# Residual cells made from both sides on TensorE in a cross-attention and spline-FFN kernel

## The reference

```python
def attn(teacher_logits, feat, Wq, bq, Wk, bk):
    query = einsum('bnc,dc->bnd', feat, Wq) + bq
    key = einsum('bnc,dc->bnd', feat, Wk) + bk
    attention = softmax(einsum('bnd,bmd->bnm', query, key))
    return einsum('bln,bmn->blm', teacher_logits, attention)

def spline(cp, out_size, in_size):   # p0..p3: four neighbouring control points, f: place between them
    w = 0.5 * (2*p1 + (p2-p0)*f + (2*p0-5*p1+4*p2-p3)*f**2 + (3*p1-p0-3*p2+p3)*f**3)
    return w.reshape(out_size, in_size)

x = x + attn(layernorm(x), ctx, Wq, bq, Wk, bk)
h = layernorm(x)
x = x + (silu(h @ gate_w.T) * (h @ up_w.T)) @ down_w.T
```

## Time and profile before

| | us |
|---|---|
| median of 3 runs | 286.06 |
| lowest and highest | 284.72, 287.19 |
| the profiled execution | 285.89 |
| its span | 283.9 |
| mean granted TensorE clock, share of full | 0.976 |

### The profile page before, as it was taken

The page is one execution under the profiler, slowest core; times in us unless marked ns, Lnnn a source line. Parts: engine busy times, 40 slices in busy tenths (PEclk is TensorE's granted clock), DMA queues, the critical chain, the costliest instruction groups (busy, mean ns, idle before and its releaser), DMA issues.

```text
span 283.9 us, 3824 instructions
## 1 busy us (share of the span) xinstructions
PE 263.8 (93%) x1250; PEld 168.4 (59%) x1252; DVE 182.0 (64%) x322; ACT 125.2 (44%) x202; POOL 132.9 (47%) x138
## 2 busy tenths in 40 slices
PE   7699479997999999999999999999999999599995
PEld 3232167763654858865548588755375888364674
DVE  0699977887457774764567838646587476464403
ACT  3044623325767702257767222557674133353300
POOL 0489462579653811309718123078083131594800
PEclk9959959999999999999999999999999999999999
DMA  6899044000720000032600000226000001100003
GB/s 188 312 424 409 2 131 168 0 2 0 267 105 0 3 0 0 2 148 90 279 0 0 0 0 0 94 76 274 0 0 0 0 0 74 74 0 2 0 0 148
DMA packets 7209, 23.23 MB, mean 82 GB/s; under 512 B 1184, under 2 KB 2336, under 8 KB 5792
## 3 DMA queue, kind: packets, MB, share of 16 engines
q1 hardware_dynamic: 7200, 23.11, 21.7%
HBM read 18.92 MB, written 4.19 MB: 81 GB/s over the span
## 4 chain that ended last, share of the span: by engine, by line
PE 73%; DVE 13%; ACT 5%; issue 4%; DMA 2%; POOL 1%; SPq 1%; ACTq 0%; DVEq 0%; POOLq 0%
PE bank L1304 11%; PE bank L1350 10%; PE bank L1306 9%; PE bank L1324 7%; PE bank L1157 5%; PE bank L1254 5%; PE bank L1255 4%; PE bank L1256 4%; PE bank L1168 4%; PE bank L1357 3%; DVE prod L856 3%; PE bank L1211 3%; DMA power<-in_g_power 2%; DVE prob L840 2%; DVE inter L947 1%
## 5 line engine op out<-in xcount | busy, mean ns | idle before, releaser
L1107 POOL TENSOR_TENSOR ih<-inter,ones 128x512 fp32r<-128x512 f32 x64 | 65.7, 1042 | 35.2 <-DVE inter L947 33.7
L947 DVE TENSOR_TENSOR inter<-inter,bank 128x512 f32<-128x512 f32 x64 | 43.4, 687 | 26.0 <-ACT inter L762 26.0
L762 ACT ACTIVATE inter<-bank 128x512 f32<-128x512 f32 x64 | 37.7, 599 | 25.1 <-PE bank L1306 24.5
L733 ACT ACTIVATE qk<-bank,nmr,rstd 128x512 f32<-128x512 f32 x16 | 12.5, 780 | 46.7 <-PE bank L1256 46.7
L1350 PEld LDWEIGHTS bank<-d_r,ih 128*128 128x128 f32 x256 | 30.6, 192 | 4.1 <-issue 3.2
L1304 PE MATMUL bank<-xh,gate_r 128*128 128x512 f32 x64 | 29.9, 467 | 1.5 <-DVE zg L939 1.5
L1350 PE MATMUL bank<-d_r,ih 128*128 128x192 f32 x256 | 31.1, 274 | 0.0
L1324 PE MATMUL bank<-inter,d_u 128*64 128x512 f32 x128 | 30.1, 602 | 0.0
L1304 PE MATMUL bank<-xh,up_r 128*128 128x512 f32 x64 | 27.2, 425 | 1.4 <-DVE inter L947 1.3
L1091 POOL TENSOR_TENSOR xres<-x,ones 128x2048 f32<-128x2048 f32 x4 | 14.4, 3602 | 23.9 <-DMA out<-xres 23.6
L1306 PE MATMUL bank<-zg,gate_v 102*128 102x512 f32 x64 | 25.3, 395 | 0.0
(11 more groups left out here) (100 smaller groups left out, 458.2 us busy)
## 6 DMA issues: line engine op xcount, KB each, us to landing
x<-in_x SPq DMA_DIRECT2D x4, 1024.0 KB, 4.8
xT<-in_xT SPq DMA_DIRECT2D x4, 1024.0 KB, 6.9
out<-xres SPq DMA_DIRECT2D x16, 256.0 KB, 2.1
ctxT<-in_ctxT SPq DMA_DIRECT2D x4, 512.0 KB, 7.6
rd<-in_d_r SPq DMA_DIRECT2D x2, 768.0 KB, 6.4
knots<-in_d_knot SPq DMA_DIRECT2D x1, 1280.0 KB, 12.1
d_coef<-in_d_coef SPq DMA_DIRECT2D x1, 1024.0 KB, 14.8
d_pt<-in_d_node SPq DMA_DIRECT2D x1, 1024.0 KB, 16.9
```

The source lines that it names most:

```text
L762: nc.scalar.activation(inter[:, m], gbank[m % 2][:], ACT.Silu).then_inc(s["silu_done"], 1)
L947: V.tensor_tensor(inter[:, m], inter[:, m], ubank[m % 2][:], ALU.mult).then_inc(s["mult_done"], 1)
L1107: G.tensor_tensor(ih[:, m], inter[:, m], ones[:, 0].broadcast_to([P, TOK]), ALU.mult).then_inc(s["ih_done"], 1)
```

## The change

- Each cell is now made as two polynomials, one for the side in front of the break and one for the side behind it, both by float32 products with 32 rows on TensorE (gate and up straight from `weighted`; down from a table `d_table` of factors times jumps). `residual` on VectorE is one `copy_predicated` within PSUM, by a loaded byte mask, and on ScalarE one copy into the weights. GpSimd has no part in it any more. `spread(r)` makes cells r and r + 1 in one step.
- The bf16 splits go. GpSimd makes the low part of `x` for batch 0 (`split_x0`), the tables (`tables`, six operations of 128x512) and all of `down_nodes`. `powers` moves to VectorE.
- `project` leaves the head of `ffn`. For batch 0 it stands in the prologue ahead of `residual(10)`; for batches 1 to 3 at the end of the turn before. `replicate` opens `ffn`; it no longer lies inside `qk`.
- `normalise` of the last tile is a step of its own (`normalise_last`). The prologue has another order with `qk(0)` first, four `keep_warm` of which none comes later, and the loads are in another order, context and query weights first. The loads `r2g`, `r3g`, `rd2`, `rd3`, `g_pick`, `d_spread` give way to `g_cell`, `g_after`, `d_table`, `d_shape`, `d_after`.

```diff
 def attention_only(st):
     st.constants()
...
+    for _ in range(4):
+        st.keep_warm(zdbank)
+    st.qk(0)
+    st.powers(0)
+    st.spread(0)
+    for t in range(2):
+        st.energy(0, t)
+    st.residual(0)
+    for t in range(2):
+        st.softmax(0, t)
+    for u in range(2):
+        st.node_product(u)
+    st.residual(1)
+    st.node_weights(0)
+    st.powers(1)
+    for t in range(2, 4):
+        st.energy(0, t)
+    st.softmax(0, 2)
+    st.node_weights(1)
+    st.softmax(0, 3)
+    st.spread(2)
+    for n in range(NT):
+        st.split_x0(n)
+    for u in range(2, 4):
+        st.node_product(u)
+    st.scale(0)
+    for t in range(2):
+        st.prob_t(0, t)
+    st.residual(2)
+    st.split_prob(0, 0)
+    st.residual(3)
+    st.split_prob(0, 1)
+    st.node_weights(2)
+    st.jump_inputs(0)
+    for t in range(2, 4):
+        st.prob_t(0, t)
+        st.split_prob(0, t)
+    st.spread(4)
+    st.node_weights(3)
+    st.stats(0)
+    st.xm(0, 0)
+    for u in range(4, 6):
+        st.node_product(u)
+    st.jump_inputs(1)
+    for r in range(4, 6):
+        st.residual(r)
+    st.mean_shift(0)
+    st.xm(0, 1)
+    st.spread(6)
+    st.node_weights(4)
+    st.add_xm(0, 0)
+    st.node_weights(5)
+    st.xm(0, 2)
+    st.jumps()
+    st.tables()
+    for u in range(6, 8):
+        st.node_product(u)
+    for r in range(6, 8):
+        st.residual(r)
+    st.add_xm(0, 1)
+    st.xm(0, 3)
+    for u in range(6, 8):
+        st.node_weights(u)
+    for t in range(2, 4):
+        st.add_xm(0, t)
+    st.spread(8)
+    st.residual(8)
+    st.normalise_last(0)
+    st.residual(9)
+    st.spread(10)
+    st.turn()
+    for t in range(4):
+        st.norm_t(0, t)
+        st.cast_t(0, t)
+    for k in range(4):
+        st.down_taps(k)
+    st.down_nodes()
+    st.project(0)
+    for r in range(10, 12):
+        st.residual(r)
+    st.spread(12)
+    for r in range(12, 14):
+        st.residual(r)
+    st.spread(14)
+    for r in range(14, 16):
+        st.residual(r)
 def ffn(st, b, a=None):
-    st.project(b)
-    if a is not None:
-        st.between(a)
-    else:
-        st.replicate(b)
+    st.replicate(b)
...
     if a is not None:
         st.cast_t(a, 3)
+        st.project(a)
# VectorE and ScalarE, residual
-    V.tensor_tensor(prod2[:, r % 2, k, 0:width], bank[2 * (r % 2) + k][:, 0:width], part[...], ALU.mult)  # k = 0, 1
+    V.copy_predicated(left, after, right).then_inc(s["picked"], 1)
+    act.wait_ge(s["picked"], r + 1)
+    nc.scalar.activation(dst, bank[2 * (r % 2)][:, 0:dst.shape[1]], ACT.Copy).then_inc(s["res_done"], 1)
# TensorE, spread
+    if r == 2 * CLS:
+        pe.wait_ge(s["table_done"], SIDES)
+        pe.wait_ge(s["shape_in"], 16)
+    for side in range(SIDES):
+        for q in (r, r + 1):
+            if side == 0 and q >= 2:
+                pe.wait_ge(s["res_done"], q - 1)
+            dst = bank[2 * (q % 2) + side]
+            if q < 2 * CLS:
+                c = slice(q % CLS * WROWS, (q % CLS + 1) * WROWS)
+                last = mm(dst[:], g_cell[c, side], weighted[c, q // CLS], start=True, stop=True)
+            else:
+                for n, m in enumerate(tile_pair(q)):
+                    w = m // CLS
+                    c = slice(QUAD * w, QUAD * (w + 1))
+                    last = mm(like_blocks(dst[:, n * STRIP:(n + 1) * STRIP], w), d_shape[c, side, m % CLS],
+                              in_blocks(d_table[c, 0, side], w), start=True, stop=True)
# GpSimd, tables
+    for k in range(2):
+        pool.wait_ge(s["jump_done"], k + 1)
+        for side in range(SIDES):
+            G.tensor_tensor(d_table[:, k, side], d_table[:, k, side], jump[:, k], ALU.mult)
+    for side in range(SIDES):
+        pool.wait_ge(s["table_mul"], 2 + side + 1)
+        G.tensor_tensor(d_table[:, 0, side], d_table[:, 0, side], d_table[:, 1, side], ALU.add)
```

More of the change, by code:

```diff
@@ L55 @@
 WIDTH = PERIOD / 4
-S2, S3 = 256.0, 2048.0
 EPS = 1e-5
@@ L154, in constants @@
     coef = np.zeros((CLS, WROWS, G_K))
+    cell_coef = np.zeros((CLS, POWERS, TAPS, SIDES, P))
+    after = np.zeros((P, CLS, HID), np.uint8)
     jump = {2: np.array([0.5, -1, 0, 1, -0.5]), 3: np.array([0.5, -2, 3, -2, 0.5])}
-    pick = np.zeros((CLS, POWERS, TAPS, 2, P))
-    r2, r3 = np.zeros((P, INTER)), np.zeros((P, INTER))
     for a in range(CLS):
         h = hidden[a * P:(a + 1) * P]
-        for n in range(4):
-            for k, scale in enumerate((S2, S3)):
-                pick[a, 0:2, n:n + 5, k] += jump[2 + k][:, None] / scale * (cell[h] // CLS == n)
         i = rows[a].ravel()
         place = ((knot[i] + (cell[h] // CLS)[:, None]) - start[i]) * PERIOD
-        left, right = nodes[cell[h]][:, None], nodes[cell[h] + 1][:, None]
-        r2[:, a * HID:(a + 1) * HID], r3[:, a * HID:(a + 1) * HID] = cell_residual(h[:, None], left, right, place)
+        left, right = nodes[cell[h]], nodes[cell[h] + 1]
+        if not ((place > left[:, None]) & (place < right[:, None])).all():
+            raise ValueError("a break outside its cell")
+        after[:, a] = h[:, None] > place
         phase = start[i] - knot[i]
@@ L170, in constants @@
         power[a] = ((phase - mid) / half) ** np.arange(POWERS)[:, None, None]
+        for j in range(P):
+            n = cell[h[j]] // CLS
+            for side, polys in enumerate(gate_cell(h[j], left[j], right[j], n, mid, half)):
+                for k, poly in enumerate(polys):
+                    cell_coef[a, 0:len(poly.coef), n:n + 5, side, j] += poly.coef[:, None] * jump[2 + k]
         for n in range(G_NODES):
@@ L370, in attention_only @@
-            for t in range(3, 7):
-                st.keep_warm(t)
-            for r in range(2):
-                st.spread(r)
+                st.softmax(0, t)
[10 more added lines that the diff above has]
+            st.spread(2)
@@ L1153, in qk @@
                     for n in range(2):
-                        if n == 1 and not first(b):
-                            Stages.replicate(b - 1)
                         for c in range(CTX // P):
@@ L1192, in spread @@
-                    for k in range(2):
-                        dst = bank[2 * (r % 2) + k]
-                        if r < 2 * CLS:
-                            c = slice(r % CLS * WROWS, (r % CLS + 1) * WROWS)
-                            last = mm(dst[:], pick[c, k], win_hl[c, r // CLS], start=True, stop=True)
-                        else:
-                            for n in range(2):
-                                m = 2 * (r - 2 * CLS) + n
-                                for part, row in pieces(dst[:, n * STRIP:(n + 1) * STRIP], jump[k], m // CLS):
-                                    last = mm(part, spread_[:, m], row, start=True, stop=True)
```

456 lines of the change are left out of this document (197 added, 259 removed).

## The result

| | before | changed |
|---|---|---|
| median of 4 runs, us | 286.6 | 309.3 |
| lowest and highest | 284.7, 287.2 | 308.0, 309.9 |
| ratio, 95% interval | | 1.081 (1.077 to 1.085) |
| profiled execution, its span | 285.89, 283.9 | 308.66, 306.6 |
| mean granted clock | 0.976 | 0.916 |

The direction was forecast, the size was not: 291.0 was said, and 309.3 lies outside 284.5 to 295.5. The span has grown by 22.7 us, 16.9 of them ahead of the first gate product and 5.8 behind it (212.7 us from there to the end before, 218.5 now).

A forecast was written before the change was run, and what follows sets the result against it. TensorE bounds the loop, hand-overs between engines the prologue. Span 283.9 + 2.0 (first gate product later, 1.3 of it clock) + 3.1 (heads of turns) = 289.0, plus 2.0 outside the span: 291.0 us, range 284.5 to 295.5.

The forecast's parts named there:

- ledger: Prologue: the queues run step by step in written order at full clock; first gate product at 71.9 us against 71.2.
- rival 3: Prologue picks: each costs 1.3 us instead of 0.69, source and target both in PSUM; time 297; chance 0.07.
- Rival 4: Prologue: the lead survives, first gate product at 67.0, time 284.8; chance 0.30, of which 0.12 more than 1% faster.
- The clock: Prologue: half clock behind TensorE gaps of 2.6 and 2.4 us; 1.3 us taken, ends 0 and 5.1.
- second fall: Prologue: half clock from the 2.4 us gap ahead of spread(10), on spread(10), transposes and project; about 2.7 us more.
- G: Start of the first gate product, end of the prologue: 71.2 us before, forecast 71.9 + 1.3 = 73.2.
- first fall: Prologue: half clock from the 2.6 us gap ahead of the transposes; 2.4 us passed on, half of it taken.
- The ledger of the middle: Prologue, 24 to 50 us: named likeliest error, if VectorE and ScalarE wait less for each other than counted.
- The port: Prologue: GpSimd's tables share a port pair with VectorE's additions of x and last jump; up to 1.4 us more.
- The heads of the turns: Loop, batches 1 and 2: TensorE idles 1.53 us each ahead of replicate, 3.06 in all; 3.1 taken.

The follow-up runs named there:

- e2: The run with fills: changed kernel plus 50 idle products of ones on TensorE in the five long gaps of the prologue; 301.3 us.
- e4: Changed kernel plus six idle products of ones on either side of replicate in batch 3; 305.8 us.
- e5: Changed kernel with replicate woven into qk again, GpSimd's low parts of x behind the scaling, idle products in batch 3 and the prologue; 294.9 us.
- e10: Changed kernel with replicate woven, low parts of x behind the scaling, tables early, last cells ahead of project, idle products at batch 3's head only; 294.9 us.
- e11: e10 plus idle products of ones in the prologue, around the node products, between the transposes and ahead of spread(10); 295.4 us.
- e7: Changed kernel with picks 10 and 11 and spread(12) directly behind spread(10), picks 12 and 13 among the transposes, spread(14) ahead of project; 301.5 us.
- e3: Changed kernel with one wait more: GpSimd begins the low parts of x only when VectorE has scaled the softmax; 304.3 us.
- e6: Kernel before with project moved to the end of the turn before and replicate at the head, no longer inside qk; 293.8 us.
- e12: e6 plus six idle products of ones ahead of each replicate and six more behind it in batch 3; 290.9 us.
- e13: Changed kernel with e3's wait, jump_inputs(1) directly behind jump_inputs(0), and GpSimd's down taps and down_nodes behind VectorE's low part of zp; 303.6 us.
- e14: e5 with 6 idle products in the first gap, the two additions of e13, and no idle products between the transposes; 294.4 us.

## Why the prediction was wrong

**The frame was right.** The kernel's loop is bound by TensorE, the prologue by hand-overs, and the loss comes from both. The ledger's first 21 us stand: `qk(0)` at 6.1 as said, the last exponential at 21.5 (21.9 said), a gate `spread` 1.99 (2.2), a down `spread` 2.04 at full clock (2.2), the pick 0.69 and 0.55 (0.69, 0.55; rival 3 falls). The picks held up by queue positions, `spread(8)` waiting for the tables and `spread(12)` for cells 10 and 11 are all in the timeline. Rival 4, the lead survives, falls: the scaling ended at 26.5 against a forecast of 23.9 and 37.05 before, a lead of 10.5 us in place of 13, and all of it was lost.

**The step that failed first is "The clock".** I priced it at 1.3 us with ends 0 and 5.1, "since one row can't say how short a gap is harmless". The run with fills measured 8.0, of which 6.9 are in the prologue, and e4 3.4 in batch 3, where I had not looked at all, since the kernel before went through the same gaps at full speed. Three things were missed. The gap of 2.6 us ahead of the transposes was 5.4. The second fall came behind another gap than the one I had: 3.0 us ahead of `spread(8)`, for the tables, where the ledger has 0.7, while ahead of `spread(10)` it was 1.3 and not 2.4. And a third, 2.5 us ahead of `spread(12)`, stands in my own ledger (59.7 to 62.5) and was not counted as one; what e2 won behind it, 5.2 us, is the largest part. Also I let each fall last some 7 us, as in the earlier trace rows (the second there ends at 42.2, by its row, not at 42.9). Here one fall lasted 17 us (22.7 to 39.7), with further gaps inside it, the second and third 13.6 each, so 44 of the 88 us ahead of G ran at half speed. The chain passes on only what lies on it: of the first fall, the one that I priced, at most 2.5 us (below).

**The ledger of the middle failed too.** I called 24 to 50 us the place where I was most likely wrong, but thought of shorter waits. VectorE's first statistics start at 34.68 and cell 9's pick ends at 62.81:

```profile
34.68 2.46 DVE L830 BATCH_NORM_STATS2 bst<-x 128x6 f32<-128x512 f32 x4
...
62.26 0.55 DVE L868 COPY_PREDICATED bank<-d_after,bank 128x384 f32<-128x384 uint8 x1
```

and in e5, whose clock was full through the whole stretch:

```profile
33.65 2.46 DVE L852 BATCH_NORM_STATS2 bst<-x 128x6 f32<-128x512 f32 x4
...
59.31 0.55 DVE L890 COPY_PREDICATED bank<-d_after,bank 128x384 f32<-128x384 uint8 x1
```

| us | ledger | changed | e2 | e5 | e10 | e11 |
|---|---|---|---|---|---|---|
| the scaling ends | 23.9 | 26.5 | 26.8 | 24.1 | 23.4 | 24.3 |
| end of the scaling to start of the statistics | 7.5 | 8.1 | 7.5 | 9.6 | | |
| start of the statistics to cell 9's pick | 22.1 | 28.1 | 28.0 | 26.2 | | |
| end of the scaling to cell 9's pick | 29.6 | 36.3 | 35.5 | 35.8 | 34.5 | 34.5 |
| cell 9's pick to G | 18.4 | 25.3 | 18.9 | 21.0 | 22.5 | 22.5 |

(In e10 and e11 the statistics stand behind the jumps and the tail has the order of e7, so they compare with each other only. A pick counts by its end.) Up to the statistics the ledger is right in e2, at full clock, and 0.6 are clock. From the statistics to the pick, 4.1 us more than the ledger are there at full clock, and only 1.9 can be clock. Behind the pick it is the other way round: with the clock nearly full the ledger is right to 0.5 us, and 6.4 are clock. What makes the 4.1 no run has shown. The rows suggest where: in e5 as in the changed kernel, the reciprocal root of tile 0 starts the tables 1.7 us behind the first jump, the six table operations take 8.8 us instead of 7.5, and the mean shift 1.2 instead of 0.17, in e5 about 4 in all by my estimate, and each of them runs beside work of the other engine.

**The port was named and put in the wrong place.** I weighed it at the tables, up to 1.4 us. The ledger itself has the low parts of `x` on GpSimd beside the four scalings, and priced the scalings at 1.68. They took 4.71, and e3 shows 5.0 us for that one meeting, 3.0 of it directly. At the tables it is 1.3 (six operations 8.8 us against 7.5), about what I had named, but outside the forecast. The section of the Trainium skill that the prediction cited (SBUF — State Buffer, SBUF: two separate sides) names two kinds of VectorE operation that need the shared ports, one with two SBUF inputs and one in a two-port mode. I used the first; the scaling, float32 from SBUF to SBUF, behaved as the second would.

**The heads of the turns** were right where costed: 1.44 us twice, 2.9 of 3.1. Their size in a run alone (e6, 7.9, of which 5.7 stay in e12) shows what was left out of the price, the half clock that a gap may bring.

**The sum.** From 291.0 to 309.3 are 18.3 us, of which 0.7 is the distance of the profiled execution from the median. In the spans 17.6 are left, 14.9 ahead of G and 2.7 behind it. Ahead of G: clock 8.9 (0.6, 1.9 and 6.4) less the 1.3 taken, 7.6; the scaling 2.6 late, by the port; steps that the ledger had too short, 4.6 (4.1 as above, 0.5 in the tail). Behind G: clock 3.0, heads -0.2. The single runs do not add up, and the table says why. e5 has the edits for clock, port and heads, and the ledger without any of them would give 285.9 + 0.7 = 286.6; it came to 294.9. Its G is 80.8 in place of 71.9: 2.1 because its products of ones, at half speed, held up the first transposes, the same 4.1 in the middle, and 2.6 in the tail, where the clock was at half from 61.3 to 71.4. No run kept the clock full up to G, and none took the 4.1 apart; e13 and e14, with GpSimd's other operations but the tables out of the way, show no gain, both with half clock near the mean shift that they made short.

## What to carry to other kernels

Price an idle gap of TensorE twice: by its length, and by half speed (here 7 us of it in the loop, 14 to 17 in the prologue) on what follows, and then ask which of it TensorE's own work passes on: 17 us of half clock in the middle of the prologue cost at most 2.5 us, 13.6 at its end some 5. Removing filler products in the name of an order that looks tight is a change of its own, and needs its own sum; here 50 useless products made the kernel 8 us faster. When work moves to GpSimd, list what VectorE does from SBUF at that very time and put a wait between the two if the VectorE step is on the chain: one added wait gave 5 us. And a woven pair (half a `qk` for each wait) that is unwoven for order's sake costs its gap in every turn of the loop.

## What the runs showed of the hardware

Half clock behind a gap is not a fixed matter: the same two gaps of 1.53 and 1.47 us left the clock full in the kernel before, brought 6.8 us of half speed in the changed kernel, and none in e7. What decides it no run shows. Executions of one kernel differ in it too: the four of e6 have mean clocks of 0.976 to 0.952 and times of 290.7 to 295.2 us. The products of ones that should keep the clock up take twice as long once it has fallen (eight in 3.59 us where eight took 1.90 at full clock), and then delay the work that they were to speed up.

Four float32 scalings on VectorE from SBUF to SBUF took 4.71 us beside GpSimd operations and 1.67 without; a VectorE operation of four columns took 1.23 beside one and 0.17 without; a cast of 512 columns 1.26 and 0.43. GpSimd's own operations grew by a tenth in the first of these meetings (4.95 to 5.49), and two tiny ones ahead of the tables took 1.81 and 1.01 us, where the next pair took 0.18 and 0.55. The Trainium skill (SBUF — State Buffer, Who interferes with whom) says that a VectorE operation in a two-port mode and a GpSimd operation exclude each other for the whole instruction. The direction agrees. The size doesn't quite: exclusion for all of both would take 1.67 + 4.95 = 6.62 us from the first start to the last end, and they took 5.84 (21.83 to 27.67).

`copy_predicated` within PSUM, 512 float32 columns with a byte mask, takes 0.69 us, the same as the product of a bank with an SBUF tile in the earlier trace rows.
